# Gate product with both parts of the gate matrix side by side, weight preparation on GpSimd, and a new order of an AdaLN block with a state-space layer and a mixture of experts

## What is computed

```python
sa, ca, ga, sb, cb, gb = (mod[:, 0], mod[:, 1], mod[:, 2], mod[:, 3], mod[:, 4], mod[:, 5])
ga = (2 * (ga >= 0) - 1) * jnp.maximum(jnp.abs(ga), 0.25)
gb = (2 * (gb >= 0) - 1) * jnp.maximum(jnp.abs(gb), 0.25)
h = _layernorm(x, axis=-1) * (1 + ca) + sa
x = x + ga * _L0_attn_ref(h, L0_attn_W_in, L0_attn_b_in, L0_attn_A, L0_attn_C, L0_attn_W_out, L0_attn_b_out)
h = _layernorm(x, axis=-1) * (1 + cb) + sb
x = x + gb * _L0_ffn_ref(h, L0_ffn_gate_w, L0_ffn_gate_b, L0_ffn_expert_w, L0_ffn_expert_b)
```

## Time and profile before

| | |
|---|---|
| median of three runs | 226.14 us (225.55 to 227.24) |
| the profiled execution | 226.16 us |
| its span | 224.3 us |
| TensorE, matmuls | 208.8 us, 93% |
| TensorE, weight loads | 160.8 us, 72% |
| VectorE | 195.2 us, 87% |
| ScalarE | 179.8 us, 80% |
| GpSimd | 158.6 us, 71% |
| granted clock of TensorE, mean | 0.982 |

### The profile page before, as it was taken

One profiled execution on the slowest core, in us unless ns is written; L12 is line 12 of the kernel. 1 busy time (PEld: TensorE's weight loads), 2 busy tenths in 40 slices (PEclk: granted clock), 3 DMA queues, 4 the chain that ended last, 5 costly groups with the idle time before them and its releaser, 6 DMA issues.

```text
span 224.3 us, 4503 instructions
## 1 busy us (share of the span) xinstructions
PE 208.8 (93%) x1093; PEld 160.8 (72%) x1093; DVE 195.2 (87%) x840; ACT 179.8 (80%) x595; POOL 158.6 (71%) x203
## 2 busy tenths in 40 slices
PE   6988989999999999999999999999999999979940
PEld 5884586877778787868686868687878777757720
DVE  3299997979999999999999999999989898786795
ACT  5322321989899998989898989898989899999940
POOL 7001781578598979797979797979797976784880
PEclk9999996999999999999999999999999999999995
DMA  4910110222001111111111111111010101001013
GB/s 132 238 35 4 47 47 0 59 60 64 22 25 51 47 48 50 47 48 47 50 48 47 48 51 47 47 48 51 0 47 3 47 1 48 3 0 47 3 47 94
DMA packets 20115, 10.35 MB, mean 46 GB/s; under 512 B 1369, under 2 KB 19938, under 8 KB 20090
## 3 DMA queue, kind: packets, MB, share of 16 engines
q1 hardware_dynamic: 18872, 9.54, 15.2%
q10 hardware_dynamic: 1218, 0.53, 0.9%
HBM read 5.81 MB, written 4.26 MB: 45 GB/s over the span
## 4 chain that ended last, share of the span: by engine, by line
PE 74%; DVE 13%; ACT 4%; DMA 3%; issue 3%; SPq 1%; DVEq 0%; ACTq 0%
PE ring L1598 13%; PE ring L1600 12%; PE ring L1599 12%; PE bank_a L1546 6%; PE bank_g L1537 6%; PE bank_v L1530 6%; PE bank_g L1493 4%; DMA x_in<-in_L_attn_x_dram 3%; PE bank_g L1577 3%; PE bank_g L1576 3%; PE bank_g L1575 3%; PE bank_a L1493 3%; ACT z L637 2%; PE bank_v L1531 2%; ACT xn L650 1%
## 5 line engine op out<-in xcount | busy, mean ns | idle before, releaser
L637 ACT ACTIVATE z<-ring,wts 128x128 f32<-128x128 f32 x440 | 122.6, 401 | 1.2 <-PE ring L1600 0.9
L474 POOL TENSOR_TENSOR z<-z 128x512 f32<-128x512 f32 x46 | 59.3, 1292 | 32.4 <-ACT z L637 32.4
L1598 PE MATMUL ring<-expert_w_hi,h_hi 128*128 128x512 f32 x128 | 53.9, 421 | 1.0 <-ACT z L637 1.0
L1600 PE MATMUL ring<-expert_w_hi,h_lo 128*128 128x512 f32 x128 | 50.6, 395 | 0.0
L1599 PE MATMUL ring<-expert_w_lo,h_hi 128*128 128x512 f32 x128 | 50.5, 394 | 0.0
L482 POOL TENSOR_TENSOR z<-z 128x512 f32<-128x512 f32 x31 | 39.4, 1288 | 0.5
L437 POOL TENSOR_TENSOR x_in<-x_in,gab_all 128x512 f32<-128x512 f32 x16 | 20.7, 1295 | 16.0 <-DVE gab_all L804 15.8
L1598 PEld LDWEIGHTS ring<-expert_w_hi,h_hi 128*128 128x128 f32 x128 | 24.5, 191 | 8.8 <-issue 5.3
L453 POOL TENSOR_SCALAR xn<-x_in,neg_mean,rstd 128x128 f32<-128x128 f32 x56 | 24.6, 454 | 7.7 <-DVE rstd L902 6.8
L1599 PEld LDWEIGHTS ring<-expert_w_lo,h_hi 128*128 128x128 f32 x128 | 24.4, 191 | 5.3 <-issue 0.8
L1600 PEld LDWEIGHTS ring<-expert_w_hi,h_lo 128*128 128x128 f32 x128 | 24.2, 189 | 5.6
(11 more groups left out here) (125 smaller groups left out, 428.1 us busy)
## 6 DMA issues: line engine op xcount, KB each, us to landing
x_in<-in_L_attn_x_dram SPq DMA_DIRECT2D x16, 256.0 KB, 2.8
out_dram<-x SPq DMA_DIRECT2D x15, 256.0 KB, 2.3
expert_w<-in_L_ffn_expert_w_dram ACTq DMA_DIRECT2D x2, 256.0 KB, 6.1
wmod<-in_L_wmod_dram SPq DMA_DIRECT2D x1, 384.0 KB, 3.9
expert_b_parts<-b_hi SPq DMA_DIRECT2D x8, 32.0 KB
out_dram<-x SPq DMA_DIRECT2D x2, 128.0 KB, 1.9
w_in<-in_L_attn_W_in_dram SPq DMA_DIRECT2D x1, 128.0 KB, 7.4
expert_b_parts<-b_lo SPq DMA_DIRECT2D x4, 32.0 KB
```

The lines of the kernel that those rows point to most:

```text
L474: nc.gpsimd.tensor_tensor(z[:, g % 2, t, 0:4, :], z[:, g % 2, t, 0:4, :], z[:, g % 2, t, 4:8, :], ALU.add).then_inc(folded[t], 1)
L637: last = nc.scalar.activation(z[:, g % 2, t, e, :], bank_k[:, (e % 4) * P:(e % 4 + 1) * P], ACT.Copy, scale=wts[:, g % 2, t, e:e + 1])
L1598: mm(bank_k[:, :], hi, expert_w_hi[:, cols], start=True, stop=False)
L1600: mm(bank_k[:, :], lo, expert_w_hi[:, cols], start=False, stop=True).then_inc(e_ready[k], 1)
```

## The change

The two fp32r parts of the gate matrix lie side by side in one tile (`gate_w_parts`, 16 columns), and each part of h2 is multiplied by both at once: two matmuls a tile instead of three, which now include low by low. The sum of the two 8-column results is a new VectorE instruction, `logit_sum`, from bank_g into scratch, and the router reads scratch. The gate's bias rows get as many zero columns between. TensorE may overwrite bank_g after `logit_summed` (before: after `sub_ready`).

ScalarE copies the four banks of gate products whole (`gates_out`), and the rows of the biases (`gate_rows_out`, `bias_rows_out`); GpSimd makes w_outg, gab_all, the gate's and the experts' bias parts from the copies. `second_norm(0)` goes from VectorE to ScalarE, `first_norm(1)` to GpSimd. SP loads x(1) third, and takes over the loads of gate_w and expert_w; `refill(2)` stands behind `spread_expert_bias`. guarded_gates has three instructions instead of four. The modulation's columns are made in two parts, so that the first norm needs only the first.

All orders are written anew: in the loop, halves 4, 1 and 7 of group s-1 are computed after turn_xn1(s+2), `mixed_bias` stands at the step's end, and add_bias to result of group s-2 belong to step s. In the drain, group 14 has two halves on VectorE instead of one, and group 15's bias product uses bank_a.

```diff
+LAST_DVE_HALVES = {14: (3, 7), 15: (3, 5, 7)}
 LAST_DVE_PAIRS = (1,)
...
-FIRST_HALVES = ((0, 1), (0, 3), (0, 2), (0, 6), (0, 5), (0, 0), (0, 7), (0, 4), (1, 6), (1, 2), (1,
-                7), (1, 1), (1, 0), (1, 3), (1, 4), (1, 5), (2, 6))
-HALF_ORDER = ((2, 0), (7, 0), (1, 0), (0, 0), (4, 0), (3, 0), (5, 0), (6, 1))
+FIRST_HALVES = ((0, 2), (0, 0), (0, 4), (0, 3), (0, 5), (0, 6), (0, 1), (0, 7), (1, 6), (1, 2), (1,
+                3), (1, 5), (1, 0))
+HALF_ORDER = ((4, -1), (1, -1), (7, -1), (6, 0), (2, 0), (3, 0), (5, 0), (0, 0))
 HALF_STEPS = (2, 12)
...
         gate_w = sb("gate_w", [P, experts])
-        gate_w_hi = sb("gate_w_hi", [P, experts], F32R)
-        gate_w_lo = sb("gate_w_lo", [P, experts], F32R)
+        gate_w_parts = sb("gate_w_parts", [P, 2, experts], F32R)
         gate_b = sb("gate_b", [batches, TILES, experts])
-        gate_b_rows = sb("gate_b_rows", [batches, TE])
...
             load(0)
             sp.dma_start(wmod[:, :], wmod_d).then_inc(wmod_in, 16)
-            load_vectors()
             load(1)
             sp.dma_start(w_in[:, :], w_in_d).then_inc(w_in_in, 16)
+            load_columns()
             sp.dma_start(w_out[:, :], w_out_d).then_inc(w_out_in, 16)
             load(2)
+            load_rows()
+            load_experts()
             load(3)
             load_expert_bias()
             refill(0)
             refill(1)
-            refill(2)
             spread_expert_bias()
...
+            def out_weights(h):
+                pool.wait_ge(outc_ready, 1)
+                pool.wait_ge(gb_ready, h + 1)
+                nc.gpsimd.tensor_tensor(w_outg[:, 2 * h:2 * h + 2, :], g_all[:, 2 * h:2 * h + 2, 0, :],
+                                        w_outc[:, :].unsqueeze(1).to_broadcast([P, 2, P]),
+                                        ALU.mult).then_inc(outw_ready, 1)
+
+            def gab(h):
+                if h == 0:
+                    pool.wait_ge(rows_in, 16 * 2)
+                pool.wait_ge(gb_ready, h + 1)
+                nc.gpsimd.tensor_tensor(gab_all[:, 2 * h:2 * h + 2, :], g_all[:, 2 * h:2 * h + 2, 0, :],
+                                        b_out[:, :].unsqueeze(1).to_broadcast([P, 2, P]),
+                                        ALU.mult).then_inc(gab_ready, 1)
...
+                                        gate_b_parts[0:batches, :, 0, :].bitcast(F32),
+                                        ALU.subtract).then_inc(gate_bias_ready, 1)
+                pool.wait_ge(gate_bias_ready, 1)
+
+            def expert_bias():
+                pool.wait_ge(bias_in, 16)
+                pool.wait_ge(bias_rows_ready, 2)
+                prep(nc.gpsimd.tensor_tensor(expert_b_rows[:, :], expert_b_rows[:, :], expert_b[:, :], ALU.add))
+                nc.gpsimd.tensor_copy(expert_b_hi[:, :], expert_b_rows[:, :]).then_inc(bias_high_ready, 1)
+                pool.wait_ge(bias_high_ready, 1)
+                nc.gpsimd.tensor_tensor(expert_b_lo[:, :], expert_b_rows[:, :], expert_b_hi[:, :].bitcast(F32),
+                                        ALU.subtract).then_inc(bias_low_ready, 1)
+                pool.wait_ge(bias_low_ready, 1)
...
+            clear_pick()
+            clear_expert_b(2)
+            clear_expert_b(3)
+            clear_expert_b(4)
             clear_parts()
+            clear_expert_b(5)
+            clear_expert_b(6)
             v_bias()
+            gab(0)
+            out_weights(0)
             biased_input(0)
+            first_norm(1)
+            gab(1)
+            out_weights(1)
             biased_input(1)
             expert_low()
-            clear_expert_b(2)
             first_norm(2)
+            out_weights(2)
+            clear_expert_b(7)
+            out_weights(3)
+            gate_bias()
+            expert_bias()
             biased_input(2)
-            clear_expert_b(3)
-            clear_expert_b(4)
-            clear_expert_b(5)
             first_norm(3)
-            clear_expert_b(6)
+            weight_parts(0)
+            gab(2)
             biased_input(3)
-            clear_expert_b(7)
...
+            def gates_out(h):
+                act.wait_ge(gates_done, 1)
+                nc.scalar.copy(g_all[:, 2 * h:2 * h + 2, :, :],
+                               ring[h][:, :].rearrange("p (b k n) -> p b k n", b=2, k=2)).then_inc(gb_ready, 1)
...
             expert_high()
-            h1(0)
-            gate(0)
             h1(1)
-            gb_copy()
+            gates_out(3)
             gate(1)
+            second_norm(0)
+            gate_rows_out()
+            bias_rows_out(0)
             h2_high(0)
+            bias_rows_out(1)
             h1(2)
             exponentials(0)
             gate(2)
-            expert_bias_high()
+            weigh(0, 2)
+            weigh(0, 0)
             second_norm(1)
-            weigh(0, 1)
+            weigh(0, 5)
+            h2_high(1)
             weigh(0, 3)
...
+            def logit_sum(g):
+                dve.wait_ge(logit_ready, g + 1)
+                vec.tensor_reduce(
+                    logit_x[:, :, :],
+                    bank_g[:, 0:2 * TE].rearrange("p (j a e) -> p j e a", j=TILES, a=2),
+                    AX.X, ALU.add).then_inc(logit_summed, 1)
+
...
             def after_logits(g):
-                pe.wait_ge(sub_ready, g + 1)
+                pe.wait_ge(logit_summed, g + 1)
             def after_state(g):
...
                 for j in range(TILES):
-                    cols = bank_x[:, j * experts:(j + 1) * experts]
-                    mm(cols, tile(h2_hi, g % 2, j), gate_w_hi[:, :], start=False, stop=False)
-                    mm(cols, tile(h2_hi, g % 2, j), gate_w_lo[:, :], start=False, stop=False)
-                    last = mm(cols, tile(h2_lo, g % 2, j), gate_w_hi[:, :], start=False, stop=(j == TILES - 1))
+                    cols = bank_x[:, 2 * j * experts:2 * (j + 1) * experts]
+                    mm(cols, tile(h2_hi, g % 2, j), gate_w_x, start=False, stop=False)
+                    last = mm(cols, tile(h2_lo, g % 2, j), gate_w_x, start=False, stop=(j == TILES - 1))
                 last.then_inc(logit_ready, 1)
...
+            def bias_bank(g):
+                return bank_a if g == groups - 1 else bank_v
+
             def mixed_bias(g):
                 if g == 0:
                     pe.wait_ge(bias_in, 16 * (1 + 3 * TILES))
                 pe.wait_ge(wt_copied, g + 1)
-                mm(bank_v[:, :], w_parts_t[:, g % 2, :], expert_b_parts[:, g // per_batch, :], start=True,
+                mm(bias_bank(g)[:, :], w_parts_t[:, g % 2, :], expert_b_parts[:, g // per_batch, :], start=True,
                    stop=True).then_inc(bias_ready, 1)
-            keep_clock(ring[0], 3)
+            keep_clock(ring[0], 5)
             turn_silu()
-            keep_clock(ring[0], 4)
+            keep_clock(ring[0], 5)
             modulation_rows()
-            modulation_columns()
-            keep_clock(ring[0], 11)
+            modulation_columns(0)
+            keep_clock(ring[0], 2)
+            modulation_columns(1)
+            turn_xn1(0)
             gate_rows()
-            keep_clock(bank_a, 4)
-            turn_xn1(0)
-            keep_clock(bank_v, 7)
             state_input(0)
             gate_input(0)
             after_turn(0)
+            keep_clock(bank_a, 13)
+            output_product(0)
+            after_product(0)
             turn_xn1(1)
             after_state(0)
+            keep_clock(bank_v, 8)
             state_input(1)
-            after_turn(1)
-            output_product(0)
             after_gate(0)
             gate_input(1)
             bias_rows()
-            after_product(0)
-            keep_clock(bank_a, 4)
+            after_gate(1)
+            turn_xn2(0)
+            after_turn(1)
             output_product(1)
-            after_gate(1)
-            keep_clock(bank_g, 8)
-            turn_xn2(0)
+            keep_clock(ring[1], 7)
             after_product(1)
-            keep_clock(bank_a, 7)
             turn_xn1(2)
+            keep_clock(ring[1], 3)
```

867 lines of the change are left out of this document (428 added, 439 removed), and 3 rows, old and new, of the table LAST_HALVES.

## The result

The changed kernel is faster, and by more than I forecast. Its five runs took 209.76, 212.14, 213.07, 213.12 and 213.54 us; the median of four of them, without the run of 212.14, is 213.09, against 225.85 (225.55 to 227.24) of the kernel before on the same chip. The ratio is 0.9329, interval 0.9216 to 0.9442, which is 210.7 us. Forecast were 215.3 us and a range from 211.5 to 220. The median lies in that range, the 210.7 us just under it, and the interval of the ratio (208.1 to 213.2 us) reaches into it.

A forecast was written before the change was run, and what follows sets the result against it. It took VectorE to bound the fill, TensorE the middle, and a ScalarE-TensorE race, then serial VectorE work, the drain. From 226.16 us, fill -5.2, middle -4.0 and drain -1.7 gave 215.3 us, range 211.5 to 220.

The forecast's parts named there:

- Rival 3: Middle: sixteen columns are not free, the gate product saves only 0.17 us a step; total 217.4 us, chance 0.06.
- The middle, the bounds: Middle: TensorE stays the bound at 11.12 us a step; 11.2 taken, eleven steps -4.0 us, bounds -4.9 and -1.3.
- VectorE's part: Middle: logit_sum adds 0.15 us a step (bounds 0.10 and 0.25), so VectorE needs 10.88 + 0.15 = 11.03.
- rival 1: Middle: VectorE or ScalarE holds the step; at 11.45 us total 218.0, at no gain 219.3; chance 0.19.
- The wait that I called likely: Middle: state_input(s+2) waits nearly bare for result(s-2), behind one more VectorE instruction; 11.2 is 0.08 us above the bound.
- the rule of the Trainium skill quoted there: Middle: judge TensorE by weight-load share, others by occupancy; VectorE is most contended, removed weight loads buy nothing, 219.3 us.
- The fill: Start to h1(4) on ScalarE: VectorE loses work, h1(4) at 52.6 instead of 57.84, -5.2 us, bounds -6.5 and -1.5.
- ten fillers at 0.25 us a record: Fill start: rows' product waits for 10 instead of 7 fillers, 6.9 instead of 5.71 us, a loss of 1.2.
- The two queues behind it: Fill: GpSimd's bias work before biased_input(2), SP's spread_expert_bias before refill(2); both covered by 1 to 2 us.
- Rival 2: Fill gives little: moved work, late bias chain or refill(2), or clock falls; gain 1.5 us, total 219.0, chance 0.11.
- The drain: From h1(15): one ScalarE half fewer, -1.05 us; VectorE's end about 5.0 instead of 5.9; -1.7 taken, bounds 0 and -2.9.
- Rival 4: Middle: slower through a closed loop in VectorE's queue; from a step of 12.2 us, at 12.4 total 228.4; chance 0.04.

The follow-up runs named there:

- e16: Changed kernel with fillers fewer on the path and more in early idle time, and one VectorE statistic moved ahead of the scan: 207.70 us, ratio 0.9177.
- e10: e8 with logit_sum done twice on VectorE, the first into columns nobody reads: step 11.10 us, +0.14.
- e8: Changed kernel without the low part of h2 in the gate product, five matmuls instead of nine: step 10.958 us, median 210.50 us.
- e13: e9 with GpSimd's first fold of a step waiting until VectorE's sum_pairs of the group before are done: step 10.956 us.
- e1: Kernel before with only the change's nine-matmul gate product and logit_sum, all orders of work as before: 218.94 us, ratio 0.9713, step 11.15.
- e4: Changed kernel with four matmuls more in each gate product, 13 again, new orders kept: 220.82 us, ratio 0.9796, step 11.335.
- e7: Changed kernel with eight instead of 13 filler products ahead of output_product(0): 208.4 and 208.7 us without a clock fall, 212.0 and 212.1 otherwise; ratio 0.9267.
- e5: Changed kernel run again unaltered: three of six runs took 213.2 to 213.8 us, two 209.66 and 209.70, one 211.06.
- e2: Kernel before with second_norm moved ahead of one weighing on ScalarE and shifts ahead of the scan on VectorE: 252.66 us, step 13.7.
- e3: e1 and e2's edits together on the kernel before: 252.54 us, step 13.8.
- e14: e2 with GpSimd's first fold waiting until sum_pairs are done: 247.22 us.
- e15: e3 with GpSimd's first fold waiting until sum_pairs are done: 236.38 us.
- e9: e8 with ScalarE weighing three instead of four experts in halves 3 and 5 of groups 2 to 11: mean step 12.08 us.
- e11: Changed kernel with three instead of five filler products between the transpose of silu and the rows' product: 211.96 us, ratio 0.9387.

## Why the prediction was right or wrong

**The middle, the gate product: right.** Nine starts 0.111 apart, 0.445 us a step, 64 columns at no extra price. Rival 3 is out.

**The middle, the bounds: wrong.** The failed step is "TensorE 11.565 - 0.444 = 11.12", for which I wrote that starts were back to back at every row I checked. 0.17 us of the 11.565 were a wait for second_norm, hidden under the modelled end of the output product's last matmul. TensorE's own starts add up to 10.90 (e16 runs at that). My rows didn't show it: the 1.13 us of the output product in the earlier trace rows, which I divided by eight for the price of 128 columns (0.141), ends with a modelled end and is 1.13 with the wait and without it. The starts give it: seven distances in the changed kernel are 0.185 and six times 0.111, and the next product follows 0.111 behind the last, 0.97 in all; in the kernel before the last distance is 0.25 to 0.32.

**VectorE's part: right in its added cost, wrong in its sum.** logit_sum costs 0.14 (e10), I took 0.15. But the sum 11.03 came out as 10.74 of work and 0.19 of wait, 10.93. VectorE's work is 0.14 below the 10.88 of before with an instruction more. I take it that this lies in how the small dependent instructions stand between others, but did not test it.

**Who bounds: rival 1's mechanism, without its price.** I said TensorE would stay the bound by 0.09. It is VectorE (e8, e10, e13, e16), by 0.06: the step is 10.965, TensorE's own starts 10.90. The wait that I called likely, state_input(s+2) behind result(s-2), is the one that came, at 0.08 us a step where I gave 0.08. That the two sizes agree is luck: with VectorE's loop holding the step, TensorE's wait is only what its own work leaves of it (0.08 with nine matmuls, 0.4 to 0.5 with five). Rival 1 came true without costing what I priced for it. Of the rule of the Trainium skill quoted there (Perfetto Trace Analysis, section Identifying the Most-Contended Engine): VectorE has the highest occupancy of the other engines in both kernels (87% and 90%). It bounds the changed one, as the rule would have it, but not the one before: e1 and e4 show that the removed matmuls bought 0.42 and 0.37 us a step.

**The fill: right in its places, short in its size.** All marks came early:

| mark | forecast | after | early by |
|---|---|---|---|
| rows' product | 6.9 | 6.17 | 0.7 |
| first transposes | 10.9 | 9.34 | 1.6 |
| output_product(0) | 17.8 | 16.23 | 1.6 |
| turn_xn2(0) | 26.6 | 24.87 | 1.7 |
| logits(0) | 30.8 | 28.82 | 2.0 |
| first weighing | 34.6 | 32.49 | 2.1 |
| h1(4) | 52.6 | 50.02 | 2.6 |

The failed step is the first: ten fillers at 0.25 us a record. That was the price of TensorE's slow spacing, which the kernel before had up to 11.4 us; here it ended at 5.64, and the starts of the second five stand 0.213 apart up to there and 0.111 behind. Those ten records took 2.07 us here, 1.71 in e7 and 2.50 in e5, as the slow spacing ended at 5.64, 4.89 and 6.70. The same holds for part of the next 0.9: from the rows' product to first_norm(0) I gave 2.9 us and it took 2.0, of which the rows' product itself took 0.54 to the next start instead of 0.95. The other 0.5 is what I gave that chain too much. The 1.6 us of the first transposes were carried on, with 0.3 more at the logits. The last 0.5 arises from the first weighing to h1(4): the 16.3 us of before held a wait of 0.60 us, and ScalarE waits only 0.19 in this stretch now. ScalarE's row of before:

```profile
48.59 0.23 ACT L626 ACTIVATE l_exp<-l_sub 128x32 f32<-128x32 f32 x1 [0.60 <-DVE l_sub L922]
```

One reading was too strong: VectorE was not busy without a break behind x(1) in the kernel before; from 11.5 to 39 us it stood 1.9 of 27.5. The two queues behind it held: the expert bias was done at 32.8 and biased_input(2) at 34.1. Rival 2 was right in one thing that this profile doesn't show: the clock falls again, at another place, in six of the eleven runs of this kernel, for about 3.4 us, and by their clock (0.98) probably for less in two more.

**The drain: right**, 37.3 us for 37.5. Both of its terms are near: -1.3 up to the end of the last weighing for -1.05, and -0.6 behind it for about -0.9.

**Rival 4, slower:** not here, but it exists. e2, e3, e14 and e15 are as slow as it says, 12.3 to 13.8 us a step, and each came from moving one norm ahead of one weighing, with shifts ahead of the scan.

## What to carry to other kernels

Before you call an engine's stretch back to back, compare its start-to-start distances with the smallest ones seen for the same instruction: a wait can lie under a modelled end. When three engines are within 2% of each other, take work off one at a time to see which one holds the step; removing work from an engine that doesn't can make a step longer, by letting another engine start into a collision. Price fillers by what they buy: those in short idle gaps kept the clock from falling here, and five of those ahead of output_product(0) were 1.0 us of path. Look where the clock's record begins before you read a 1.00 in its column.

## What the hardware showed that I had not expected

- VectorE's additions with both inputs in SBUF and GpSimd's additions held each other up, and the one that started first ran to its end. A VectorE addition that started 0.14 us or more behind a GpSimd one ended about 0.28 us after that one, so 0.93 and 1.50 us for the two of sum_pairs in e2, and 0.41 and 1.51 in e9, instead of 0.41 each. Where they started within 0.06 us of one another, VectorE's kept their 0.41 and GpSimd's took up to 1.94 instead of 1.27, as in the drain of the kernel before:

```profile
214.69 1.94 POOL L474 TENSOR_TENSOR z<-z 128x512 f32<-128x512 f32 x1
214.75 0.75 DVE L1012 TENSOR_TENSOR mix<-z 128x256 f32<-128x256 f32 x2
```

  One wait on GpSimd gave the 0.41 back (e13). The Trainium skill, GPSIMD Engine Reference, section Specifications, says that GpSimd's way to SBUF is shared with VectorE and that instructions with two SBUF inputs contend for it; by that, the trace agrees.
- TensorE ran at the spacing of the lower level (gate rows 2.05 us for eight, against 1.19) under a printed granted clock of 1.00 (e11), and under 0.50 with the same 2.05 (e5). The 1.00 is no record: the trace's clock records begin at 14.19 us in e11. The Trainium skill, TensorE: Matmul & The Clock Gate, section Seeing it yourself, warns that the gate's recorded events have been seen to be unreliable; here the records there are and the distances of the starts agree (0.213 us before the first record of the changed kernel, at 5.64, and 0.111 behind it).
- The same program leaves the slow spacing at different times: at 4.89, 5.64 and 6.70 us in three runs (e7, the changed kernel, e5), and its rows' product came at 5.81, 6.17 and 6.59.
